# DLRM tower on one core: ScalarE takes chunk 0's output of layer 0 before its copy of the second chunk's x, and the dense rows are turned in iteration 2

## The reference

```python
e = jnp.stack([tbl_f[ids[:, f]] for f in range(32)], axis=1)   # x: batch 512 x 32 fields x 16, f32
# three layers (a CIN): x0 = h = e
for i in range(3):
    z = (x0[:, :, None, :] * h[:, None, :, :]).reshape(B, F * G, E)
    y = relu(einsum('oc,bce->boe', W[i], z) + b[i][None, :, None])        # 128 output channels
    x_keep, h = (y[:, :64], y[:, 64:]) if i != 2 else (y, y)
    xs.append(x_keep)
z = sum(concatenate(xs, axis=1), axis=2)                                   # 512 x 256
h = maximum(concatenate([z, dense_ctx], axis=1) @ W_top1 + b_top1, 0)      # 272 -> 512
h = maximum(h @ W_top2 + b_top2, 0)                                        # 512 -> 256
y = h @ W_top3                                                             # 256 -> 1
```

## Time and profile before

| | |
|---|---|
| median of three runs | 567.95 us |
| the profiled execution: its own time | 571.28 us |
| its span, first to last instruction | 569.1 us |
| PE busy | 516.9 us, 91% of the span |
| DVE, POOL, ACT busy | 372.3, 192.2, 140.7 us |
| data moved by DMA | 95.62 MB, mean 168 GB/s |

### The profile page before, as it was taken

How to read it: one execution, slowest core, us unless ns; L and a number is a source line. 1 busy time by engine, 2 the same in 40 slices (tenths; PEclk the granted TensorE clock), 3 DMA queues, 4 the chain that set the end, 5 groups by cost and what they waited for, 6 DMA issues and landing times.

```text
span 569.1 us, 3811 instructions
## 1 busy us (share of the span) xinstructions
PE 516.9 (91%) x1332; PEld 253.2 (44%) x1332; DVE 372.3 (65%) x214; ACT 140.7 (25%) x211; POOL 192.2 (34%) x162
## 2 busy tenths in 40 slices
PE   0242979999999999999999999999999999999998
PEld 0131534545454545454444545454545454444446
DVE  1123468785949494949687695949494959675822
ACT  1102122414132222223141414122222213130304
POOL 5771535243352608070625344351703030300000
PEclk9985989999999999999999999999999999999999
DMA  6668977959596959788795959595969789922000
GB/s 214 154 115 216 233 183 161 251 105 247 120 249 124 250 122 234 160 193 208 158 243 123 249 123 251 123 250 108 253 133 238 156 182 252 207 51 74 9 0 0
DMA packets 46546, 95.62 MB, mean 168 GB/s; under 512 B 24464, under 2 KB 27408, under 8 KB 38080
## 3 DMA queue, kind: packets, MB, share of 16 engines
q1 hardware_dynamic: 40416, 94.16, 71.1%
q0 software_dynamic: 4096, 1.06, 1.5%
q10 hardware_dynamic: 2016, 0.17, 0.3%
HBM read 93.27 MB, written 2.10 MB: 168 GB/s over the span
## 4 chain that ended last, share of the span: by engine, by line
PE 84%; DMA 5%; another core or an unknown queue 3%; issue 2%; DVE 1%; POOL 1%; SPq 1%; ACT 1%; DVEq 0%
PE acc L577 74%; PE acc L588 7%; DMA x_scratch<-x_t 3%; DMA x_rot<-x_scratch 1%; POOL gathered L314 1%; PE acc L598 1%; SPq L265 1%; DVE z L377 1%; PE acc L593 1%; DMA row<-in_row 0%; DMA gathered<-in_table,rows_all 0%; PE acc L650 0%; PE x_bank L560 0%; PE h L650 0%
## 5 line engine op out<-in xcount | busy, mean ns | idle before, releaser
L577 PE MATMUL acc<-z,w_direct 128*128 128x512 f32 x1024 | 447.5, 596 | 22.2 <-DVE z L377 17.3
L577 PEld LDWEIGHTS acc<-z,w_direct 128*128 128x128 f32 x1024 | 194.3, 191 | 261.3 <-issue 245.3
L377 DVE TENSOR_TENSOR z<-h,x_pair 128x2048 f32<-128x2048 f32 (+1 forms) x65 | 144.9, 2250 | 138.3 <-issue 85.6
L331 POOL TENSOR_TENSOR z_low<-z,z_high 128x1024 fp32r<-128x1024 f32 x30 | 70.3, 2365 | 256.2 <-ACT z_high L467 256.2
L314 POOL DMA_INDIRECT gathered<-in_table,rows_all x128 | 121.7, 951 | 40.9 <-issue 35.2
L377 DVE TENSOR_TENSOR z<-h_odd,x_pair 128x2048 f32<-128x2048 f32 x32 | 72.2, 2279 | 7.9 <-ACT h_odd L481 7.9
L377 DVE TENSOR_TENSOR z<-h_even,x_pair 128x2048 f32<-128x2048 f32 x32 | 72.3, 2280 | 0.2 <-issue 0.2
L481 ACT ACTIVATE h<-acc,columns 64x512 f32<-64x512 f32 x32 | 20.8, 652 | 166.4 <-PE acc L588 99.5
L481 ACT ACTIVATE kept<-acc,columns 64x512 f32<-64x512 f32 (+1 forms) x48 | 32.8, 683 | 56.0 <-PE acc L577 55.2
L588 PE MATMUL acc<-z_high,w_high 128*128 128x512 f32 x64 | 27.1, 505 | 11.6 <-DVE z_low L384 11.6
L394 DVE TENSOR_REDUCE sum<-kept 128x32 f32<-128x512 f32 x32 | 32.9, 1029 | 6.6 <-ACT kept L481 6.6
(11 more groups left out here) (108 smaller groups left out, 128.8 us busy)
## 6 DMA issues: line engine op xcount, KB each, us to landing
x_pair<-x_scratch SPq DMA_DIRECT2D x128, 512.0 KB, 15.4
x_rot<-x_scratch SPq DMA_DIRECT2D x64, 256.0 KB
x_rep<-x_scratch SPq DMA_DIRECT2D x16, 256.0 KB
w_direct<-in_W SPq DMA_DIRECT2D x2, 1024.0 KB, 6.5
gathered<-in_table,rows_all POOLq DMA_INDIRECT x128
x_scratch<-x_t SPq DMA_DIRECT2D x32, 64.0 KB
x_pair<-in_W_top SPq DMA_DIRECT2D x2, 512.0 KB, 4.5
z<-in_W SPq DMA_DIRECT2D x1, 576.0 KB, 4.3
```

Of the source, the lines that this page charges most:

```text
L331: nc.gpsimd.tensor_tensor(z_low[:, slot_of(pair)], products_of(pair), z_high[:, slot_of(pair)].bitcast(F32), ALU.subtract).then_inc(low_po ...
L377: nc.vector.tensor_tensor(z[:, step.group % Z_SLOTS, first:end], h[:].unsqueeze(1).to_broadcast([P, end - first, N]), x_pair[:, chunk % 2, ...
L577: op = nc.tensor.matmul(acc[pair.layer][:], w_direct[:, first + i], products_of(pair)[:, i], start=i == 0 and pair is OPENS[pair.layer, pa ...
```

## The change

Three things move; nothing is added or taken away.

- On ACT, `layer_out(0, 0)` is called right after the first two `high_part`, ahead of `copy_x(1)`. Before, it came after `copy_x(1)` and after the rounding of the dense rows.
- On PE, the four transposes of the dense rows leave the place right after `turn_x(1)` and stand at the start of iteration 2.
- The rounding of the dense rows on ACT goes to iteration 2, place n = 0, and DVE's `dense_parts` from the end of iteration 1 to the end of iteration 2.

```diff
@@ VectorE
-                if c == 1:
+                if c == 2:
                     dve.wait_ge(dense_rounded, 1)
                     nc.vector.scalar_tensor_tensor(
                         out=dense_parts[:], ...
@@ ScalarE
                 high_part(pair)
+            layer_out(0, 0)
             copy_x(1)
-            act.wait_ge(dense_turned, 1)
-            nc.scalar.activation(dense_high[:], dense_bank[0:COPIES * EMBED, :], ACT.Copy).then_inc(dense_rounded, 1)
-            layer_out(0, 0)
             for c, steps in enumerate(PLAN):
                 for n, step in enumerate(steps):
                     if c >= 1 and n == 1:
                         layer_out(1, c - 1)
...
+                    if c == 2 and n == 0:
+                        act.wait_ge(dense_turned, 1)
+                        nc.scalar.activation(dense_high[:], dense_bank[0:COPIES * EMBED, :],
+                                             ACT.Copy).then_inc(dense_rounded, 1)
@@ TensorE
             turn_x(1)
-            pe.wait_ge(dense_here, 16 * COPIES)
-            for i in range(BATCH // P):
-                op = nc.tensor.transpose(dense_bank[...], dense_rows[:, i]..., ident[:])
-            op.then_inc(dense_turned, 1)
             for c, steps in enumerate(PLAN):
+                if c == 2:
+                    pe.wait_ge(dense_here, 16 * COPIES)
+                    for i in range(BATCH // P):
+                        op = nc.tensor.transpose(dense_bank[...], dense_rows[:, i]..., ident[:])
+                    op.then_inc(dense_turned, 1)
```

More of the change, by code:

```diff
@@ L608, in _ @@
             turn_x(1)
-            pe.wait_ge(dense_here, 16 * COPIES)
-            for i in range(BATCH // P):
-                op = nc.tensor.transpose(dense_bank[0:COPIES * EMBED, i * P:(i + 1) * P],
-                                         dense_rows[:, i].rearrange("p c e -> p (c e)"), ident[:])
-            op.then_inc(dense_turned, 1)
-            for c, steps in enumerate(PLAN):
+            for c, steps in enumerate(PLAN):
+                if c == 2:
+                    pe.wait_ge(dense_here, 16 * COPIES)
+                    for i in range(BATCH // P):
+                        op = nc.tensor.transpose(dense_bank[0:COPIES * EMBED, i * P:(i + 1) * P],
+                                                 dense_rows[:, i].rearrange("p c e -> p (c e)"), ident[:])
+                    op.then_inc(dense_turned, 1)
                 for n, step in enumerate(steps):
```

## The result

The changed kernel takes 571.84 us (median of four runs, 570.93 to 572.83) against 567.99 us (567.9 to 568.61) for the kernel before: a ratio of 1.0066, 95% interval 1.0046 to 1.0085. By the medians it is 3.9 us slower. The forecast was 571.3. Measured once more beside other kernels, the ratio was 1.0081 (1.0058 to 1.0104), and the medians were 3.9 us apart again.

The account below looks back on a forecast made before the run. PE was taken to bound the kernel behind 92 us, with transfers holding the opening. Opening 0 plus iteration 2 +3.32 us, on the median 567.95 + 3.3 = 571.3 us; range 568.7 to 573.9.

Parts of the forecast that it names:

- rival B: Iteration 2: PE's clock drops after the new stop, as after an earlier one that lost about 1.7 us; 573.0, chance 0.16.
- A: The forecast itself: 0 in the opening, +3.32 us in iteration 2; 571.3 us, own range 569.5 to 572, chance 0.51.
- (c): Opening: PE stands 1.09 us until 92.24 for DVE, held by chunk 2's x_rot behind a queued store; claimed not to move.
- the 0: Opening: forecast gain of 0, at most 1.8 us, because transfers hold the rest of the opening.
- The prediction's own sign: Opening: if DVE's two waits on transfers, at 61.63 and 87.03, moved forward by several us, F is right.
- F: Opening not held by transfers: h up to 13.9 us sooner passes on to the stream; net -10.6, 557.4; chance 0.10.
- Rival C: Opening: chunk 1's x copy slips behind layer_out(0, 0), up to 2.0 us on top of A; 572.5 to 573.3, chance 0.11.
- D: Iteration 2: ACT's long hold belongs to the dense transposes and moves along, up to 8.8 us; about 580, chance 0.05.
- E: No change, 567.95 within 1.1: the opening gives back what iteration 2 takes, 3.9 against 3.3; chance 0.07.

Follow-up runs that it names:

- Removing the wait alone: Changed kernel with ACT's dense rounding at n = 3 of iteration 2, behind layer_out(1, 1) and layer_out(2, 0): 568.67 us against the changed kernel's 571.62.
- the dense rows moved alone: Changed kernel with copy_x(1) again ahead of layer_out(0, 0), so only the dense rows move to iteration 2: 571.04 us, 1.0059 to the kernel before.
- The swap: Kernel before with only layer_out(0, 0) put ahead of copy_x(1) on ACT, dense rows left in the opening: 568.53 us, 1.0011 to the kernel before.
- dense rows in iteration 1: Changed kernel with transposes at the start of iteration 1, rounding there at n = 3, dense_parts at its end: 567.24 us, 1.0005 to the kernel before.

## Why the prediction was right, and where it was not

**Iteration 2: right, and to the size.** Forecast: 3.32 us from the transposes' start to PE's next product. Measured: 3.32. By its links: ACT 0.63 us after the first transpose (forecast 0.64), `h_odd` and kept in 2.0 us behind the rounding, PE 0.05 us behind kept (108.36 + 0.68 to 109.09), DVE's products in time. Removing the wait alone brings back 2.95 us; splitting the change puts the loss on the dense rows.

**The clock (rival B): seen in two of three profiles.** The chances had A at three times B. The granted clock after the stop of 2.73 us was 1.00 in the first profile of the changed kernel, and 0.50 in the two others that have it. Windows of the first, of its repetition and of the dense rows moved alone, columns as in the earlier trace rows:

```profile
109.20:112.40 3.20, 3.20 (x8) 1.52 (x9) 3.20 (x2) 1.70 (x3) 0.00 (x0) 1.00 0.64 136
```

```profile
109.60:112.80 3.20, 2.89 (x4) 1.34 (x5) 3.20 (x2) 2.10 (x4) 0.00 (x0) 0.50 1.03 215
```

```profile
108.20:111.40 3.20, 2.98 (x4) 1.44 (x5) 3.20 (x2) 2.00 (x4) 0.00 (x0) 0.50 0.75 161
```

From PE's start to the next turn of x it is 10.41 us in the first (109.09 to 119.50) and 11.88 in the second (109.91 to 121.79), for the same 24 records: 1.5 us, where the forecast's price was 1.7. Three executions can't give a share; with half to two thirds of them, the estimate is 3.3 + 0.8 to 1.0 = 4.1 to 4.3 us, near the 3.9 measured twice. The two executions with the low clock were also above the medians of their kernels (573.76 against 571.62, 572.29 against 571.04), the one without it was not (571.48 against 571.84).

But no run shows that the clock is what lies between 3.3 and 3.9. The swap's 0.1%, about 0.6 us, would fill it as well. The dense rows alone cost 1.0059, which is 3.3 us and leaves nothing for the clock. Removing the wait brought back 2.95 us, where 2.9 and the clock's share would make 3.7 or more. The intervals are too wide to choose; that the result came within 0.5 us of A's 571.3, with a clock price in some executions that A left out, is in part luck.

**The opening: right in its sum, wrong in its picture.** "PE starts its stream at 92.24 as before" failed: 88.93 in the changed kernel. The step that failed is the choice of the execution. Its 9.70 and 8.86 us of waiting, of which the prediction says that "no row names what held them", were taken as the kernel's own, the time of 571.28 us beside a median of 567.95 was a warning that I read only as an offset, and (c) was taken for an anchor. In the second profile of before PE is unbroken from 70.79, with (c) absent; in the changed kernel it is there with 0.56 us. What holds of it: DVE still stood for `x_pair` (2.11 us until 56.87) and for `x_rot` with `h` there long before, so transfers pace the opening, and the earlier `h` was worth nothing that can be measured (dense rows in iteration 1: 1.0005). The 10 to 14 us of stall that the change was to remove were 1.0 us in the other two profiles of that order (in the first, the copy at 35.62, `h` at 36.67). So the 0 was luck in part: with 1.0 us to win, it would have come out near 0 whatever paced the opening.

The prediction's own sign misled as well. It said that F is right if DVE's two waits on transfers move forward by several us. They did, from 61.63 to 56.87 and from 87.03 to 83.72, and F is wrong. In the second profile of before the same two products are at 56.36 and 81.51:

```profile
56.36 2.29 DVE L378 TENSOR_TENSOR z<-h,x_pair 128x2048 f32<-128x2048 f32 x1 [2.04 <-DMA x_pair<-x_scratch]
81.51 2.29 DVE L366 TENSOR_TENSOR z<-x_rep,x_rot 128x2048 f32<-128x2048 f32 x1 [3.59 <-DMA x_rot<-x_scratch]
```

The move belongs to the execution and not to the change.

**Rival C** (the slip): seen, 2.1 us from PE's turn to the copy, at a price that no run resolves, 0.1% with an interval that holds no change. **D**: no; ACT took up the dense rows 0.63 us after their first transpose, and the long holds are in none of the 13 other profiles. **E** and **F**: no; the opening gave nothing back, and the stall of 10 to 14 us that F was to pass on wasn't there.

## What to carry to other kernels

When a step that links two engines is moved, look at what stands behind it on the engine that waits, and at whether the engine waited for needs that: here ACT's rounding waited for PE, and behind it was the output that frees PE's next bank, so 1 us of work became 3.3 us on the bound engine. Here turning where PE waits anyway, or rounding behind the outputs that PE needs, took the stop away, each by itself. And before a stall is explained or removed, profile the same kernel a second time, above all when the profiled execution is slower than the median.

## What the runs showed that was not expected

- In one execution ACT saw PE's results up to 12.8 us after their modelled end; in two later profiles with the same order, within 0.1 us. The cause stays open.
- PE's gap (c) comes and goes between executions of nearly the same opening: none in the second profile of before, 0.56 us in the changed kernel and none in its repetition, 2.53 us with the dense rows moved alone.
- A stop of PE of 2.73 us was followed by the granted clock of 1.2 GHz (0.50) in two executions and by 2.4 GHz in another; after 3.21 us it was 0.50 over the whole window from 108.6 to 115.2 us in the one execution seen, and the 24 records took 13.24 us (109.53 to 122.77) instead of 10.41.
- Two ACT copies of 48 x 512 from PSUM, 0.59 us each, start 0.49 us apart.
